# Second attention: each score product written as four products of 32 columns in TensorE's four column groups

## The reference, cut to what matters

```python
x = x + _L0_xattn_ref(_layernorm(x), ctx, ...)     # first attention
x = x + _L0_ffn_ref(_layernorm(x), ...)            # gated feed-forward, fp8
x = x + _L1_xattn_ref(_layernorm(x), ctx, ctx, gamma)   # second attention
x = x + _L1_ffn_ref(_layernorm(x), ...)            # top 2 of 8 experts

def _L1_xattn_ref(q, k, v, gamma):                 # each (8, 256, 512), 8 heads of 32 rows
    qh, kh, vh = (a.reshape(B, 8, 32, 512) for a in (q, k, v))
    qk = jnp.einsum('bhdq,bhdl->bhql', qh, kh) / sqrt(32)
    sm = jax.nn.softmax(qk, axis=-1)
    ret = jnp.einsum('bhql,bhdl->bhdq', sm, vh)
    return gamma * ret.reshape(B, 256, 512)
```

## Time and profile before

| | |
|---|---|
| median of 3 runs | 758.33 us |
| profiled execution | 759.41 us |
| its span | 757.7 us |
| granted TensorE clock, mean | 0.991 |
| TensorE busy, matmuls | 716.9 us (95%), 4257 |
| TensorE weight loads | 302.8 us (40%), 4285 |
| VectorE busy | 571.8 us (75%) |
| ScalarE busy | 410.4 us (54%) |
| GpSimd busy | 364.5 us (48%) |
| scores L1538, 256 matmuls | 82.1 us |

### The profile page before, as it was taken

One profiled execution on the slowest core, in us unless ns is written; L12 is line 12 of the kernel. 1 busy time (PEld: TensorE's weight loads), 2 busy tenths in 40 slices (PEclk: granted clock), 3 DMA queues, 4 the chain that ended last, 5 costly groups with the idle time before them and its releaser, 6 DMA issues.

```text
span 757.7 us, 14381 instructions
## 1 busy us (share of the span) xinstructions
PE 716.9 (95%) x4257; PEld 302.8 (40%) x4285; DVE 571.8 (75%) x1108; ACT 410.4 (54%) x764; POOL 364.5 (48%) x356
## 2 busy tenths in 40 slices
PE   4999999999999999899999999999998898999995
PEld 2444544444444444212222223222224555555553
DVE  4689999796876868588888898899857666555553
ACT  2555454663646556258777776777776433222221
POOL 4676555113011041355765558776675664433433
PEclk9999999999999999989999999999999999999998
DMA  8999980017264498134343344453565799998985
GB/s 304 386 142 218 293 330 0 1 39 273 100 236 176 152 311 291 46 102 107 89 118 100 98 107 113 136 158 83 171 210 115 165 184 143 133 133 128 134 113 70
DMA packets 114182, 117.51 MB, mean 155 GB/s; under 512 B 54840, under 2 KB 78264, under 8 KB 113856
## 3 DMA queue, kind: packets, MB, share of 16 engines
q1 hardware_dynamic: 103008, 94.48, 43.1%
q0 software_dynamic: 10384, 22.02, 18.0%
q10 hardware_dynamic: 720, 0.13, 0.1%
HBM read 43.61 MB, written 59.56 MB: 136 GB/s over the span
## 4 chain that ended last, share of the span: by engine, by line
PE 29%; DMA 13%; issue 8%; DVE 3%; POOL 2%; POOLq 1%; ACT 1%; DVEq 0%; ACTq 0%
PE l_b L1538 9%; PE l_sm L1557 7%; PE l_pv L1549 7%; DMA out<-t_room,t_tag 6%; DMA out<-l_pvs,t_tag 4%; PE l_a L1479 3%; DMA out<-l_sums,t_tag 2%; DVE l_negm L1771 2%; PE l_b L1492 2%; PE l_b L1529 1%; DMA out<-l_r,t_tag 1%; POOLq L1230 1%; PE l_b L1486 1%; ACT t_room L1679 1%; POOL slots_x L2127 0%
## 5 line engine op out<-in xcount | busy, mean ns | idle before, releaser
L1679 ACT ACTIVATE t_room<-l_b 128x512 f32<-128x512 f32 x256 | 139.0, 595 | 35.9 <-PE l_b L1538 33.7
L1771 DVE TENSOR_REDUCE l_negm<-l_a 128x2 f32<-128x1024 f32 x64 | 75.1, 1219 | 9.4 <-PE l_a L1479 9.2
L1157 PE MATMUL l_a<-w1h,h_stack 128*128 x312 | 76.7, 314 | 3.1 <-DVE l_stack L1210 1.7
L1186 ACT ACTIVATE l_stack<-l_stack 128x352 f32<-128x352 f32 x39 | 19.4, 497 | 105.7 <-DVE l_stack L1210 104.8
L1771 DVE TENSOR_REDUCE h_negm<-l_a 128x2 f32<-128x1024 f32 x56 | 65.9, 1220 | 9.7 <-PE l_a L1479 9.6
L1549 PE MATMUL l_pv<-t_room,l_vt 128*32 128x512 f32 x512 | 69.1, 612 | 0.1
L1557 PE MATMUL l_sm<-t_room,ones_f 128*32 128x512 f32 x512 | 68.2, 604 | 0.0
L852 PE MATMUL ps_r<-f_xt,wg 128*128 128x512 fp8e4 x256 | 65.7, 379 | 0.0
L852 PE MATMUL ps_st<-f_xt,wg 128*128 128x512 fp8e4 x256 | 65.7, 379 | 0.0
L1001 POOL TENSOR_TENSOR X<-X,f_y 128x512 f32<-128x512 f32 x16 | 20.6, 1284 | 79.3 <-ACT f_y L902 79.3
L1240 POOL DMA_INDIRECT out<-t_room,t_tag x20 | 31.7, 1586 | 47.1 <-DVE t_room L1225 34.8
(11 more groups left out here) (302 smaller groups left out, 1560.4 us busy)
## 6 DMA issues: line engine op xcount, KB each, us to landing
slots_x<-empty SPq DMA_DIRECT2D x8, 2376.0 KB, 11.0
slots_x<-empty SPq DMA_DIRECT2D x7, 2112.0 KB, 16.6
h_stack<-h_wide SPq DMA_DIRECT2D x96, 64.0 KB
l_stack<-h_wide SPq DMA_DIRECT2D x96, 64.0 KB
f_stage<-in_w SPq DMA_DIRECT2D x8, 704.0 KB, 7.2
f_stage<-in_w SPq DMA_DIRECT2D x8, 512.0 KB
h_wide<-in_ctx SPq DMA_DIRECT2D x16, 256.0 KB
l_vt<-in_ctx_t SPq DMA_DIRECT2D x16, 256.0 KB, 3.1
```

The lines of the kernel that those rows point to most:

```text
L1157: mm = pe.matmul(self.HP[i % 2][:, 0:self.H], T.xt[i % T.AHEAD][:, xp * self.FC + f, :], self.w1[wp][:, bass.ds(e, 1), f * self.H:(f + 1) ...
L1679: act.activation(weights_at(u, c, h)[:, :], B[t % 2][:, :], ACT.Exp, scale=SCALE).then_inc(b_ok, 1)
L1771: dve.tensor_reduce(negm[u % 2][:, 2 * half:2 * half + 2, j], A[half][:, :, :], AX.X, ALU.max, negate=True)\
```

## The change

In `scores` the one matmul of 97 rows by 128 columns becomes four of 97 rows by 32 columns (`HU` is 4, `DH` is 32). Each takes 32 keys of the chunk as stationary operand and writes its 32 partitions of the same bank. The moving operand is the same 97 by 512 in all four. The last one alone counts up `b_ps`. The result in the bank, what waits for it and all other engines' programs stay as they are.

```diff
                 wait(pe, b_ok, t - 1)
-                pe.matmul(B[t % 2][:, :], stack[u % 2][0:M0 + 1, 0, h, c * P:(c + 1) * P], stack[u % 2][0:M0 + 1, 1, h, :],
-                          start=True, stop=True).then_inc(b_ps, 1)
+                for k in range(HU):
+                    rows_of = slice(DH * k, DH * k + DH)
+                    mm = pe.matmul(B[t % 2][rows_of, :], stack[u % 2][0:M0 + 1, 0, h, c * P + DH * k:c * P + DH * k + DH],
+                                   stack[u % 2][0:M0 + 1, 1, h, :], start=True, stop=True)
+                mm.then_inc(b_ps, 1)
```

## The result

The changed kernel's median is 752.99 us over 9 runs (748.95 to 756.73), beside 758.91 for the kernel before (755.49 to 760.48, 9 runs): ratio 0.9923, interval 0.9906 to 0.9940, so 5.9 us less. The profiled execution took 751.65 us. Its second attention takes 249.12 us from its first score to its end, against 255.63; a second profile of the same kernel gives 250.13. The part after it takes 183.00 us (183.14 before). The part ahead of it is 1.1 us shorter in this profile (317.79 for 318.91), which the change does not touch.

A forecast was written before the change was run, and what follows sets the result against it. TensorE's own rate was taken to set the regular unit's 15.69 us. A gain of 11.5 us less 3.0 (VectorE) and 0.5 (scatters) gave 8.0 us, so 750.5 us; forecast alone 748 to 753.5, full range 746.5 to 757.

The forecast's parts named there:

- The arrangement: TensorE, scores beside P and R: each change of array arrangement costs 0.10 to 0.12 us, and some of them go.
- Rivals C and D: Scores: four bf16 matmuls not side by side, +160 us, 2%; or arrangement still changes before P, +4 to +6 us, 6%.
- The pair: One pair of cycles on TensorE in the second attention: falls by 0.20 us, from 3.40 to 3.20.
- ScalarE's margin: Next cycle's second score: exponentials allow it at 1.59 us, it would come at 1.63; if not, 0.03 per pair.
- Weight loads: Three more loads per score on TensorE: cost 0, at worst 0.01 us per score, 2.6 us in all.
- Instruction count: TensorE's front in a regular unit: 321 loads and matmuls in 14.9 us, one per 46 ns, cost 0.
- VectorE, -3.0: Second attention: TensorE's waits for banks that VectorE's reductions must empty take back 3.0 us.
- Rival A: Second attention: VectorE holds the stage more than counted, so only -3 us, 756.4 or 755.3 us; chance 13%.
- Scatters, -0.5: Around GpSimd's scatters ScalarE and VectorE start late: 0.17 us less room per place, five units, two counted already, 0.5 us.
- The count of pairs: Units 0 to 14 of the second attention: 57 pairs gain 0.20 us each, 11.5 us.
- Unit 15: 0, tail as a whole: Unit 15 buys at most 0.2 us, counted 0; the chain after 574.5 us moves as a whole.

The follow-up runs named there:

- e1: Each score as two matmuls of 64 columns in place of four of 32, against the kernel before: 761.76 us, 1.0055.
- e2: Only the second score of each cycle split in four of 32, the first left whole, against the kernel before: 756.84 us, 0.9973.
- e7: The changed kernel with each score as eight matmuls, four column groups by two halves of the queries: 762.42 us, 1.0053 to the kernel before.
- e12: The changed kernel with maxima over half of the scores and without the sixteen scatters of rows 0 to 7: units 9 to 13 take 74.06 us against 78.82.
- e3: The changed kernel with SyncE's load of unit 3's keys issued ahead of unit 1's values and turned maxima: 750.42 us, 0.9891 to the kernel before.

## Why the prediction was right, and where it was not

The forecast (750.5, faster) holds in direction and range: 752.99 by the median, 5.9 us where some 7.8 had been put. The mechanism was right; several terms of the sum were mis-sized and some were missing, and the errors partly cancelled. Before anything is taken off, the change could give 14.1 us, where 11.5 had been put; 7.6 were taken back, where 3.5 had been put. That the number still fell inside the range is in part luck.

- *The arrangement.* Right. S to P lost its 0.10 (0.21 to 0.23 now), P to S lost it too, and e1 and e2 show that it follows the arrangement and not the splitting. Rivals C and D are out: four bf16 matmuls run beside one another at 0.22 to 0.23 a score. The Trainium skill, "TensorEngine Tiling (Array Packing)", section "Key Properties", says that a change of tiling mode drains TensorE. e1 and e2 agree in that a price appears at just these places; between 32 columns and 64 or 128 it is about 0.1 us.
- *The pair: 3.20 put, 3.10 measured.* The term was 0.20 and is 0.30. Two sizes were off. A restart of 7 ns per column group was charged to each score and does not exist (S to S stayed at 0.23), and P and R were taken to keep their 0.45 + 0.45, but run at 0.86. So the unit fell by 0.94 and not 0.80.
- *ScalarE's margin.* That it "just holds" was wrong: the second score of the next cycle comes 0.06 us late (0.29 for 0.23), twice the 0.03 that was named as the price.
- *A wait that I did not name.* Once in a unit `row_sums` waits for ScalarE's copy of the sums of the unit before. After the change (ScalarE's copy, then TensorE):

```profile
399.46 0.60 ACT L1693 ACTIVATE l_sums<-l_sm 128x512 f32<-128x512 f32 x1
```

```profile
400.12 0.64 PE L1560 MATMUL l_sm<-t_room,ones_f 128*32 128x512 f32 x4
```

  The second score started at 399.63, so R would have come at 399.86; it comes at 400.12, 0.06 after the copy's end. This is 0.26 us a unit, about 4 us in all, and is contained in the 14.75. ScalarE now has 3.4% + 4.2% of the chain of unit 5, where the earlier trace rows has TensorE alone:

```profile
by line: PE l_sm L1560 24.7%; PE l_b L1540 24.7%; PE l_pv L1552 17.5%; PE l_a L1479 11.0%; PE l_b L1492 6.7%; ACT t_room L1682 4.2%; PE l_b L1529 4.0%; issue 3.6%; ACT l_sums L1693 3.4%; PE l_b L1486 2.2%; ACTq L28 0.2%
```

- *Weight loads, 0.* Right: no place on TensorE's path shows one; Q to S after an uncovered load stayed at 0.32 (0.33 before). The Trainium skill, "TensorEngine Tiling (Array Packing)", on feature incompatibilities, denies column tiling the fast weight load. A load of 97x32 takes 93 ns in unit 5, and one of 97x128 took 96 before, so a quarter of the columns is not loaded sooner; but no gap of this trace shows a loss from it. The 5.4 us that the prediction estimated by this rule lie nearer to the measured 5.9 than its own 7.8. That is chance: what is missing lies in units 0 to 2 and 9 to 13, and not at the loads.
- *Instruction count, 0.* Right, with room: e7 runs regular units at 33 ns an instruction. What e7 loses elsewhere is open. The prediction's use of the Trainium skill, "TensorE: Matmul & The Clock Gate", section "Back-to-back issue gap", took the wrong figure: its 81 ns are for matmuls that stream 128 columns, and these stream 512, for which it gives 131 ns. Sixteen pairs would then be an estimated 2.10 us and would bind. The trace decides otherwise: S, S and P take 0.23 + 0.21 + 0.86 = 1.30 us.
- *VectorE, -3.0.* Too large. Where it alone holds (units 8 and 12) it took back 0.30 and 0.46 us more than before; units 3 to 8 together lost 0.16 of 5.64. I had charged every pair since the last near wait; most of that time VectorE was ahead again before the wait came. Rival A is out: in a regular unit TensorE has no wait for the maxima.
- *Scatters, -0.5.* This step failed most. I charged 0.17 us a place at five places, of which three counted. In units 9 to 13 the change can give 4.7 us and gave 1.6 and 0.3; with VectorE relieved 0.84, so 3.9 are lost, and e12 has 4.76 us back when they go. Where the exponential starts 1.7 to 1.8 us after the second scatter, before the change and after it, what TensorE has saved ahead of it is lost. I had taken that for a little less room. That it is so at every pair is not shown.
- *The count of pairs, from unit 0 on.* The 10 pairs of units 0 to 2 were counted as gained. Three units could give 2.8 us and became 1.35 longer: SyncE's transfers for unit 2 end there, which only the view of SyncE's queue shows and I had not followed, and the clock falls with the wait. Both terms are missing from the sum. e3 returns 3.7 us of units 0 to 2.
- *Unit 15: 0, tail as a whole.* Unit 15 fell by 0.25 (17.04 to 16.79), the tail by 0.14.

The same sum with the measured sizes: 15 units x 0.94 = 14.1; less 4.2 (units 0 to 2), 0.2 (3 to 8), 3.1 (9 to 13), 0.4 (14), plus 0.25 (15): 6.5 us, the difference of the two stages.

## What to carry to other kernels

Where matmuls of different arrangements alternate, give the small ones the arrangement of their neighbours, even at four times the instructions: each change that goes returns about 0.1 us, if both sides of it agree. Before counting such a gain over a whole stage, look for what does not move with the engine that becomes faster: a queue's chain of transfers at the start, an indirect DMA in the middle; each can swallow what was saved ahead of it. A wait that becomes visible can cost more than its length: here the granted clock fell to 0.50 with it in three of six profiles. Here one load issued earlier on SyncE (e3) was worth more with the change (0.9891 for 0.9939 beside it) than without (0.9989).

## What the runs showed of the hardware

- Column groups of 32 columns in bf16 follow one another at no measurable cost: four take 0.22 to 0.23 us over 512 columns, what one matmul of 128 takes, and eight over two halves of 256 columns likewise (0.11 a half). Groups of 64 don't spare the change to 32 (e1: 0.32 us from S to P).
- The change of arrangement is paid at each side: 0.10 us from S to P, and up to 0.14 from P's first pass to the next score.
- TensorE took 448 loads and matmuls in 14.77 us in a regular unit of e7, 33 ns each, where 320 take 14.75.
- Around a pair of indirect DMAs of GpSimd ScalarE starts late on what TensorE has finished, in the longest cases 1.7 to 1.8 us after the second one's start (units 10 and 13 after the change: 1.68 and 1.75). Without the DMAs (e12) units 9 to 13 take 4.76 us less.
- When TensorE had stood still for 2.1 to 2.4 us ahead of unit 2, its granted clock was 0.50 for 3.41 us in three profiles; after 2.0 to 2.5 us in three others it stayed at 1.00. Unit 2 took 15.0 to 15.1 us with the fall and 13.5 without.
- One small transfer of 4 KB landed 4.0 us after its issue in the profile of the changed kernel and 2.50 in that of the kernel before, the same transfer in the same place; a chain that ends in one moves by as much.
